# A deformable convolution on four engines: the entry of its rounds in another order, row distances on ScalarE, one half's third group added whole on GpSimd

## The reference

```python
def _dcnv4(t, H, W, Wv, bv, Wom, bom, Wo):
    value = (t @ Wv + bv).reshape(N, H, W, G, Cg)
    om = (t @ Wom + bom).reshape(N, H, W, G, 3 * K)
    offset = om[..., :2 * K].reshape(N, H, W, G, K, 2)
    mask = om[..., 2 * K:]
    loc_y = ys + ky + offset[..., 1]
    loc_x = xs + kx + offset[..., 0]
    sampled = _bilinear_gather(value, loc_y, loc_x)
    out = (sampled * mask[..., None]).sum(axis=4)
    return out.reshape(N, L, C) @ Wo

t = _dcnv4(t, ...)
y = relu(_bn(t, gamma, beta))
t = _dcnv4(y, ...)
y = _bn(t, gamma, beta) + shortcut
```

## Time and profile before

| what | value |
|---|---|
| median of 3 runs | 439.18 us (437.82 to 440.41) |
| profiled execution | 438.85 us |
| its span, first to last instruction | 437.1 us |
| busy PE / DVE / ACT / POOL | 384.5 / 346.4 / 286.5 / 165.9 us |
| chain of waits that ended last | DVE 27%, PE 25%, ACT 10%, issue 6%, POOL 2% |
| granted TensorE clock, mean | 0.996 |

### The profile page before, as it was taken

The page is one execution under the profiler, slowest core; times in us unless marked ns, Lnnn a source line. Parts: engine busy times, 40 slices in busy tenths (PEclk is TensorE's granted clock), DMA queues, the critical chain, the costliest instruction groups (busy, mean ns, idle before and its releaser), DMA issues.

```text
span 437.1 us, 9881 instructions
## 1 busy us (share of the span) xinstructions
PE 384.5 (88%) x3978; PEld 260.9 (60%) x3978; DVE 346.4 (79%) x673; ACT 286.5 (66%) x500; POOL 165.9 (38%) x154
## 2 busy tenths in 40 slices
PE   6988989989898897999988888989879889899887
PEld 5856842222236755666667666666659686555575
DVE  3878788899983477999998778999996676899541
ACT  4755286999926567888761678787821537898471
POOL 6000500000000048899995348999982050000000
PEclk9999999999999999999999999999999999899999
DMA  8200040000015000000000000000000000000000
GB/s 295 121 3 1 0 94 1 0 1 1 1 35 229 1 1 1 2 1 3 1 0 1 2 1 1 2 1 1 2 2 0 1 0 2 2 1 1 1 2 26
DMA packets 1630, 9.30 MB, mean 21 GB/s; under 512 B 208, under 2 KB 976, under 8 KB 1104
## 3 DMA queue, kind: packets, MB, share of 16 engines
q1 hardware_dynamic: 1440, 8.59, 5.6%
q10 hardware_dynamic: 144, 0.07, 0.1%
HBM read 7.40 MB, written 0.26 MB: 18 GB/s over the span
## 4 chain that ended last, share of the span: by engine, by line
DVE 27%; PE 25%; ACT 10%; issue 6%; POOL 2%; DVEq 0%; ACTq 0%; POOLq 0%
DVE SMT L931 7%; PE bank L1375 6%; DVE PRD L912 6%; DVE wb L912 6%; PE bank L1055 4%; ACT RINGS L629 4%; PE bank L1513 2%; PE bank L1493 2%; DVE SMT L923 2%; DVE XN L696 1%; ACT RINGS L646 1%; PE bank L1358 1%; POOL RINGS L377 1%; ACT RINGS L564 1%; PE bank L1198 1%
## 5 line engine op out<-in xcount | busy, mean ns | idle before, releaser
L1375 PE MATMUL bank<-VB,RINGS 64*128 64x144 f32 x1152 | 95.5, 299 | 18.0 <-DVE wb L912 7.3
L1375 PEld LDWEIGHTS bank<-VB,RINGS 64*128 64x128 f32 x1152 | 76.3, 186 | 43.6 <-issue 19.6
L345 POOL TENSOR_TENSOR HY<-OM,cst 128x324 f32<-128x324 f32 x32 | 23.2, 748 | 114.2 <-DVE LXA L898 114.2
L1055 PE MATMUL bank<-cst 128*128 128x128 f32 x446 | 60.1, 283 | 0.0
L1055 PEld LDWEIGHTS bank<-cst 128*128 128x128 f32 x446 | 55.4, 196 | 3.0 <-issue 2.5
L564 ACT ACTIVATE RINGS<-bank,cst 128x768 f32<-128x768 f32 x48 | 42.8, 891 | 17.4 <-PE bank L1358 17.3
L912 DVE TENSOR_TENSOR PRD<-bank,HY 128x864 f32<-128x864 f32 x48 | 50.3, 1051 | 4.7 <-PE bank L1375 4.2
L912 DVE TENSOR_TENSOR wb<-bank,HY 128x864 f32<-128x864 f32 x48 | 50.4, 1050 | 4.0 <-PE bank L1375 3.4
L567 ACT ACTIVATE RINGS<-RINGS,cst 128x768 f32<-128x768 f32 x48 | 44.9, 936 | 1.6
L1306 PE MATMUL bank<-RINGS,cst 128*32 128x512 f32 x336 | 40.7, 594 | 5.6 <-DVE RINGS L841 2.0
L518 ACT ACTIVATE RINGS<-PRD,wb 128x2048 f32<-128x2048 f32 (+1 forms) x21 | 39.4, 1919 | 5.3 <-PE bank L1306 4.2
(11 more groups left out here) (261 smaller groups left out, 709.8 us busy)
## 6 DMA issues: line engine op xcount, KB each, us to landing
wd<-in_wd SPq DMA_DIRECT2D x1, 2793.0 KB, 9.6
wb<-in_wb SPq DMA_DIRECT2D x1, 2112.0 KB, 10.0
wc<-in_wc SPq DMA_DIRECT2D x1, 1027.0 KB, 12.2
cst<-in_cst SPq DMA_DIRECT2D x1, 766.0 KB, 5.4
PRD<-PRD SPq DMA_DIRECT2D x1, 324.0 KB, 3.5
PRD<-PRD SPq DMA_DIRECT2D x1, 323.9 KB, 6.0
PRD<-PRD SPq DMA_DIRECT2D x1, 323.8 KB, 6.4
XC<-in_x SPq DMA_DIRECT2D x2, 128.0 KB, 2.3
```

The source lines that it names most:

```text
L1055: pe.matmul(bk[:, 0:P], ident, ident, start=True, stop=True)
L1375: ins = pe.matmul(view(bank[q % 2 * 2 + gp], k3 * NR, [[3 * NR, 2 * CG], [1, NR]]), view(HX, b % 2 * HXN + (3 * t + k3) * NPIX + half * P, ...
```

## The change

It has these parts.

1. **Sums.** For half 1 of images one to seven POOL adds all 864 elements of the third group instead of 432, and DVE sums that half in two reductions (L966, L973) instead of three. `PIECES` has five entries, for u = 0 to 4; image eight keeps six (`LAST_PIECES`), the first of them behind its own u = 5.
2. **Row distances.** Those of images five to eight are made on ACT, for all four images at once and one row at a time: nine instructions of 288 elements each (`rows_apart`, L572) that take the place of POOL's L345 and ACT's absolute value for these images. Five go between the hats of image three and four between those of image four. HY is no longer double-buffered: each image has its own place.
3. **Entry.** Image one's row weights are made group by group on POOL and ACT; POOL makes the distances of images two, three and four at the entry, between the masks of image one. DVE runs `points` for images five to eight in two parts: L894 and L895's successors behind u = 3, the other three behind u = 5. PE transposes image two's positions behind product 2 instead of 0.
4. **Normalised copies.** `xnc_ready` is signalled per half. The router (`top2`), `expert_choice` and the offsets of images one to four start on the first half. The router's bias matmul goes ahead of the wait. The fifth norm uses another bank of PSUM.

```diff
-PIECES = ((0, 0), (0, 1), (1, 0), (1, 1), (0, 2), (1, 2))
+PIECES = ((0, 0), (0, 1), (0, 2), (1, 0), (1, 1))
+LAST_PIECES = ((0, 0), (0, 1), (1, 0), (1, 1), (0, 2), (1, 2))
+ROWS_AFTER = {(2, 1): (0, 3), (2, 2): (3, 5), (3, 0): (5, 7), (3, 1): (7, 9)}
...
-NORM_BANKS = (7, 3, 1, 5, 5, 5, 1, 5)
+NORM_BANKS = (7, 3, 1, 5, 3, 5, 1, 5)
...
-        HY = sb("HY", 2 * 2 * HYN)
+        HY = sb("HY", B * 2 * HYN)
```

POOL's `last`:

```diff
-                second, third = (view(prd(i, half), t * TRIO, [[1, TRIO // GP]]) for t in (1, 2))
+                n = TRIO if half and b + 1 < B else TRIO // GP
+                second, third = (view(prd(i, half), t * TRIO, [[1, n]]) for t in (1, 2))
```

POOL's list of a round:

```diff
-                rows_off(turn, 0)
-                masked(turn, 0)
+                for trio in range(3):
+                    rows_off(turn, 0, trio)
+                masked(turn, 0, 0)
+                for trio in (1, 2):
+                    rows_off(turn, trio)
+                    masked(turn, 0, trio)
+                rows_off(turn, 3)
                 for b in range(B):
-                    if b + 1 < B:
-                        rows_off(turn, b + 1)
                     pairs(turn, b, 0)
                     if b + 1 < B:
                         masked(turn, b + 1)
```

ACT's new function and its list of a round:

```diff
+            def rows_apart(turn, rows):
+
+                act.wait_ge(lxa_ready, pointed(turn, B4))
+                for r in range(*rows):
+                    ins = act.activation(view(HY, B4 * 2 * HYN + r, [[HYN, 2 * B4], [NR, 3], [3 * NR, 3 * G]]),
+                                         view(LY, B4 * 2 * KG, [[KG, 2 * B4], [3 * G, 3], [1, 3 * G]]), ACT.Abs, scale=-1.0,
+                                         bias=cv("yg", 1, r))
+                ins.then_inc(hy_apart, 1)
...
                     if b == 0:
                         points_out(i)
-                        rows_hat(i)
-                    hats(i, 0)
-                    if b > 1:
-                        rows_hat(i)
-                    hats(i, 1)
-                    if b + 1 < B:
+                        for t in range(3):
+                            rows_hat(i, t)
+                            hats(i, t)
                         points_out(i + 1)
-                    hats(i, 2)
-                    if b == 0:
                         rows_hat(i + 1)
+                        continue
+                    for t in range(3):
+                        hats(i, t)
+                        if t == 0 and b > 1:
+                            rows_hat(i)
+                        if t == 1 and b + 1 < B:
+                            points_out(i + 1)
+                        if (b, t) in ROWS_AFTER:
+                            rows_apart(turn, ROWS_AFTER[b, t])
```

DVE's list of a round:

```diff
                         sample(i, *divmod(u, 2))
-                        if b:
+                        if b and u < len(PIECES):
                             sums(i - 1, *PIECES[u])
-                        if b == 0 and u == 1:
-                            points(B4, B4)
+                        elif b == B - 1:
+                            sums(i, *LAST_PIECES[0])
+                        if b == 0 and u == 3:
+                            points(B4, B4, last=False)
+                        if b == 0 and u == 5:
+                            points(B4, B4, first=False)
```

PE's `top2` (in `expert_choice` likewise, per half) and the place of image two's transpose:

```diff
-                pe.wait_ge(xnc_ready, nx)
...
+                    pe.wait_ge(xnc_ready, 2 * nx - 1 + g // 2)
...
-                points_at = {0: 1}
+                points_at = {2: 1}
```

90 lines of the change are left out of this document (57 added, 33 removed).

## The result

The changed kernel took 442.02 us (median of 20 runs, 441.27 to 447.36), the kernel before 439.25 us on the same chip in the same session (20 runs): a ratio of 1.0077, 95% interval 1.0050 to 1.0104. The forecast was 431.6 us, range 425.5 to 438.0, so it was wrong in sign and the time lies outside the range. Eleven of the 20 runs lie between 441.27 and 442.07 us, at a mean granted clock of 0.981, and nine between 443.50 and 447.36, at 0.965 to 0.977. The profiled execution of the changed kernel took 441.27 us, with a span of 439.4 us against 437.1 before and a mean granted clock of 0.981 against 0.996.

The account below looks back on a forecast made before the run. DVE and POOL were taken as both full in the middle of a round (9.91 and 9.96 of 10 us). -7.2 - 2.4 + 0.9 + 1.5 = -7.2 us from 438.85 gave 431.65, predicted as 431.6 us, range 425.5 to 438.0.

Parts of the forecast that it names:

- Middle of a round: Sums and distances, images two to seven: an image takes 8.45 us, 0.58 less; -7.2 us over two rounds.
- Normalised copies: Routers, expert_choice and first offsets: PE's idle gaps waiting for the second half of XNC go; -2.4 us.
- End of a round: Image eight's one fewer sum ends DVE about 0.5 us sooner, but PE's idle matmuls hide it; 0 us.
- the floor: End of a round: PE's 16 idle matmuls, 234.67 to 238.40, don't get shorter and hide DVE's gain.
- The entry: Start of each round: moved points meet busy POOL and some wait; +1.5 us first round, +0.9 second.
- the first rival: Entry: L894 and L897, with one input, are held up as well; 2.3 us a round, 436.2 us; chance 0.27.
- The test that the prediction set: Entry: wrong if image two's first sample starts more than 12.5 us behind image one's.
- 11.4 by the sum: Entry: the forecast itself put image two's first sample 11.4 us behind image one's.
- The clock: Entry, within the first rival: up to 438 us if PE, idle for some 5 us, loses clock.
- The distances on ScalarE: Images three and four: rows_apart at 0.39 us each; 1.2 us too much over two images, covered by ACT's free time.
- `rows_apart` are slow: ACT's distances, writing with a step of nine: at 0.95 us each 439.6 us, at 1.2 us 444; chance 0.07.

Follow-up runs that it names:

- the shorter tail: Changed kernel with late points and wrongly portioned row distances, 13 idle matmuls instead of 16 at the end of a round: 436.62 us, against 438.48 with 16.
- the bench: Changed kernel plus, behind its last instructions, seven VectorE forms alone and beside GpSimd additions and four ScalarE row-distance forms: 464.29 us.
- late points: Changed kernel with the five points instructions of images five to eight as one piece behind image two's second sample: 434.01 us, ratio 0.9836 to the kernel before.
- the idle matmuls: Changed kernel with 18 idle matmuls on TensorE behind the values of images five to eight in each round: 438.92 us, ratio 0.9959 to the kernel before.

## Why the prediction was wrong, point by point

- **Middle of a round: right.** 8.34 us an image for 8.45, with GpSimd busy throughout as forecast. The sums alone lose 7.5 us, so they need the distances to leave GpSimd; what the distances alone would give was not run.
- **Normalised copies: right**, 2.5 us by TensorE's timelines for 2.4, and 2.6 in the changed kernel.
- **End of a round: the floor was right, its price not.** "PE stands in its 16 idle matmuls", and "0 us": the floor held VectorE's next step back by 0.3 us a round (0.99 us idle against 0.70), more than half of the 0.5 that the missing sum would have given; the shorter tail gave it back.
- **The entry is the step that failed.** The forecast held up L935, L938 and L940, "an instruction with two SBUF inputs and a POOL instruction exclude each other", because the rows [5] showed that and none showed more. L934 and L939 have one SBUF input and took 1.06 and 1.11 us for 0.30. That is the first rival, at a chance of 0.27, and at 436.2 to 438 us it was still too small. The test that the prediction set, image two's first sample behind image one's, gave 12.75 us (11.4 by the sum, 13.7 by that rival). The rule of the Trainium skill ("SBUF — State Buffer", who interferes with whom) has both halves, two SBUF inputs, and `tensor_scalar` and copies in a two-port mode. The traces now agree with the second half too (a `tensor_scalar` 1.06 us for 0.30 in the changed kernel, a copy 2.10 us for 0.30 in the bench), as far as the times go; which mode an instruction ran in no trace shows. The row [7] that spoke for it, 288 elements in 0.30 us where L895 takes 0.46, was in front of me and I weighed it under the absence of a row.
- **The clock was priced too low.** It stood in that rival as "up to 438". TensorE fell to 0.50 in both rounds, and the samples of image two waited 1.9 us a round more than before (1.98 and 1.12 for 1.18). Holding the clock at the entry gave 3.1 us back.
- **The distances on ScalarE were the other wrong size.** 0.39 us was taken "the same element count" from a copy written side by side; the instruction takes 0.60, of which the bench puts 0.17 on the write of every ninth element. 9 x 0.2 is only 1.9 us a round, but there was no free time to cover it. The forecast found ScalarE 1.2 us over in two images of 8.45 us and covered that with the 1.7 us an image that it has free; those 1.7 us belong to an image of 9.03 us and are already used up in the comparison with 8.45. At 0.6 us a distance the same sum gives 3.1 us too much over images three and four, and ScalarE was indeed busy 19.71 of 20 us and VectorE waited 2.05. It is the rival "`rows_apart` are slow" at a price between its two bounds. That rival began to lose at 0.95 us because it left 1 us of free time standing; an estimate without it, from 7.2 us of gain and 18 distances, puts the point near 0.8.

Against the forecast a round is, by the trace of the first: 1.35 us at the points (12.75 - 11.4), 1.92 for the clock, 2.05 at image four (1.89 and 0.16), less 5 x 0.11 for shorter images: 4.8 us, and 9.5 for two if the second is taken as the first. The ends of the two rounds add 0.6. The traces give the whole: from the first offsets (151.76 us before, 150.09 now) to the first transposes behind the second round (340.77 and 344.25) the changed kernel takes 194.16 us and the kernel before 189.01, 5.2 more, where the forecast had 4.8 less. These 10.0 us stand against 10.1 from the sum. The profiled execution lies 9.7 us over the forecast; the 0.3 less are small gains of the copies, at the start and between the last two norms.

## What to carry to other kernels

Before moving a VectorE instruction that reads and writes SBUF alone, see what GpSimd does at the new place: each one can cost the rest of a GpSimd instruction, and a copy or a `tensor_scalar` with one input is no exception. Count the engine that starves behind it too: of the loss, 3.1 us were to be had back by holding TensorE's clock at the entry alone, and a few idle matmuls in gaps of 0.9 and 1.8 us took the spread between runs from 5 us to 0.6. Free time that was counted at the old pace is not there at the new one. And whatever is made later must not be waited for at the head of another engine's queue.

## What was not expected of the hardware

- VectorE's chain of all-SBUF instructions kept a GpSimd addition waiting for 2.7 us (4.66 in place of 2.0), through the rest of a chain of nine instructions one behind the other, while in the other order each copy waited for one whole addition of 2.06 us. Why the turns are taken one by one in the one case and not in the other was not tried.
- The same idle time of TensorE is followed by a fall of the granted clock in one round and not in the other: with late points it was 0.69 in 178 to 182 us of the first round behind 1.77 us idle and 1.00 at the same place of the second behind 1.80; with the idle matmuls it was 0.54 behind 1.49 us before image four of the first round and 1.00 behind 1.49 in the second.
- ScalarE writes 288 elements with a step of nine in 0.57 to 0.60 us and side by side in 0.42.
